# Attention and expert block on one core: an order of its own for the last unit, and its results taken out in halves

## The reference

```python
# x: (8, 1024, 256) float32; 16 heads of 16; RoPE on q and k
h = layernorm(x)
q, k, v = split(h @ Wqkv)                      # per head
num = exp(rot(q) @ rot(k).T / 4)               # numerators: rotated q, k
den = sum(exp(q @ k.T / 4), over all keys)     # denominators: plain q, k, all 1024 keys
attn = where(causal, num / den, 0)
x = x + (attn @ v) @ Wout + bout
h = layernorm(x)
shared = square(relu(h @ Ws1)) @ Ws2
logits = h @ Wr                                # 8 experts, top 2
prob = trunc(softmax(top two logits))          # 1 only where the softmax rounds to 1, else 0
x = x + shared + sum_e prob_e * (square(relu(h @ W1[e])) @ W2[e])
```

## Time and profile before

| | |
|---|---|
| median of 3 runs | 1724.95 us (1722.38 to 1730.55) |
| the profiled execution | 1729.71 us, of which the span of the trace is 1728.1 us |
| busy share of the span | ACT 92%, PE 88%, DVE 49%, POOL 30% |
| granted TensorE clock | 0.96 on the mean |
| last unit on ACT | 1631.79 to 1683.23 us |
| after the last exponential of scores | 1683.23 to 1728.1 us, 44.9 us |

### The profile page before, as it was taken

How to read it: one execution, slowest core, us unless ns; L and a number is a source line. 1 busy time by engine, 2 the same in 40 slices (tenths; PEclk the granted TensorE clock), 3 DMA queues, 4 the chain that set the end, 5 groups by cost and what they waited for, 6 DMA issues and landing times.

```text
span 1728.1 us, 25467 instructions
## 1 busy us (share of the span) xinstructions
PE 1517.6 (88%) x8224; PEld 588.5 (34%) x8224; DVE 852.2 (49%) x1946; ACT 1594.2 (92%) x2639; POOL 515.5 (30%) x865
## 2 busy tenths in 40 slices
PE   2988989899899989899898898999998999989985
PEld 1322323333333333333333333333333333333324
DVE  4434434754446554555446654456545554455215
ACT  1899999999999999999999999999999999999990
POOL 3223232422333232232333313332233323223110
PEclk8988999999999999999999999999999999999896
DMA  5332233331434314333333313343043332432200
GB/s 155 110 113 86 83 110 110 112 105 46 135 104 123 111 46 138 105 109 92 99 125 122 98 65 126 101 134 110 24 138 107 120 101 68 132 119 65 83 25 25
DMA packets 95005, 172.05 MB, mean 100 GB/s; under 512 B 15504, under 2 KB 82064, under 8 KB 82576
## 3 DMA queue, kind: packets, MB, share of 16 engines
q1 hardware_dynamic: 94272, 169.15, 31.5%
q10 hardware_dynamic: 592, 1.18, 0.3%
HBM read 111.55 MB, written 58.72 MB: 99 GB/s over the span
## 4 chain that ended last, share of the span: by engine, by line
ACT 66%; PE 15%; DVE 11%; issue 4%; DVEq 1%; POOL 1%; DMA 1%; SPq 0%; POOLq 0%
ACT scores L488 44%; ACT probs L498 19%; PE scores L544 4%; ACT probs L500 3%; PE side L602 3%; PE scores L551 3%; DVE rest L852 2%; PE y_ps L573 2%; DVE parts L850 2%; DVEq L789 1%; DVE raw L865 1%; DVE parts L856 1%; PE side L657 1%; DVE turned L870 1%; DVE rot L874 1%
## 5 line engine op out<-in xcount | busy, mean ns | idle before, releaser
L488 ACT ACTIVATE scores<-scores 128x1024 f32<-128x1024 f32 x1024 | 1051.5, 1041 | 37.8 <-PE scores L544 36.9
L544 PE MATMUL scores<-stack 96*128 96x512 bf16 x2048 | 591.4, 388 | 80.8 <-ACT scores L488 36.7
L498 ACT ACTIVATE probs<-scores 128x1024 f32<-128x1024 f32 x512 | 487.2, 1037 | 33.2 <-PE scores L551 32.6
L551 PE MATMUL scores<-stack 96*128 96x512 bf16 (+3 forms) x1536 | 337.1, 337 | 51.9 <-ACT scores L488 37.6
L394 POOL TENSOR_SCALAR_AFFINE_SELECT probs<-probs 128x256 f32<-128x256 f32 (+1 forms) x640 | 231.8, 387 | 426.4 <-ACT probs L498 304.8
L573 PE MATMUL y_ps<-probs,v_sb 128*32 128x512 f32 (+3 forms) x3072 | 332.8, 505 | 8.8 <-POOL probs L394 7.6
L544 PEld LDWEIGHTS scores<-stack 96*128 96x128 bf16 x2048 | 151.2, 98 | 514.1 <-ACT scores L488 236.3
L404 POOL TENSOR_TENSOR parts<-rest,parts 128x512 bf16<-128x512 f32 x124 | 143.2, 1154 | 314.7 <-DVE parts L856 314.7
L551 PEld LDWEIGHTS scores<-stack 96*128 96x128 bf16 x1536 | 124.4, 99 | 289.3 <-ACT scores L488 118.1
L488 ACT ACTIVATION_READ_ACCUMULATOR scores<-scores 128x1 f32 x1024 | 219.6, 214 | 0.0
L402 POOL TENSOR_TENSOR rot<-raw,cos_sb 128x512 f32<-128x512 f32 x62 | 89.4, 1442 | 398.1 <-DVEq L866 398.1
(11 more groups left out here) (121 smaller groups left out, 1082.8 us busy)
## 6 DMA issues: line engine op xcount, KB each, us to landing
stack<-qk_parts SPq DMA_DIRECT2D x762, 128.0 KB, 2.6
qk_parts<-parts SPq DMA_DIRECT2D x127, 384.0 KB, 2.6
out<-x_mid SPq DMA_DIRECT2D x32, 256.0 KB, 2.8
x_in<-in_L_attn_x SPq DMA_DIRECT2D x7, 1024.0 KB, 5.4
x_in<-in_L_attn_x SPq DMA_DIRECT2D x2, 512.0 KB, 4.4
stack<-qk_parts ACTq DMA_DIRECT2D x6, 128.0 KB, 4.6
probs<-in_L_attn_Wqkv SPq DMA_DIRECT2D x1, 512.0 KB, 5.7
cos_sb<-in_cos SPq DMA_DIRECT2D x1, 512.0 KB, 6.5
```

The costliest lines, as they stand in the source:

```text
L488: nc.scalar.activation(src, src, ACT.Exp, scale=SCALE, accum_out=den[:, g % 2, i, j:j + 1]).then_inc(exp_done, 1)
L498: nc.scalar.activation(probs[:, chunk % 2, j, :], src, ACT.Exp, scale=SCALE).then_inc(exp_done, 1)
L544: mm = nc.tensor.matmul(tile[:, half * HALF:(half + 1) * HALF], q[:, j, i * P:(i + 1) * P], k[:, j, half * HALF:(half + 1) * HALF], start= ...
L551: mm = nc.tensor.matmul(tile[:, col:col + n], k[:, h, i * P:(i + 1) * P], q[:, h, q0:q0 + n], start=True, stop=True)
```

## The change

**The last unit's order.** Unit 3 of batch 7 gets its own tables (`unit_of` gives it index 4): `ORDER_LAST` starts with numerators of chunk 0, and the first 16 denominators are those of the upper query blocks 4 to 7 (all four heads), the last 16 those of the lower. The upper ones are complete after step 31. Pieces with V, side work, reciprocals and branch have new steps; ffn 4 to 7 go to steps 0, 3, 8 and 17, the branch to 28.

**The upper half inside the unit.** The rest of batch 7 is now a list of 23 tiles, `END_TILES`, in halves. Its first five (norm 0, acc 2 and 3, t2 2 and 3, with the upper half's statistics and layernorm) run in `side` at steps 37, 38, 40, 47 and 49. The other 18 run after the unit, in an order that mixes both halves. The inverse root is now done twice, on 4 columns each. Logits are made in two halves.

**Outputs.** For batch 7 `send_out` does not wait for the branch any more; the pairs go out in the order 2, 3, 0, 1. If the branch is taken, DVE waits for those sends and POOL sends all four again; if not, POOL only raises `out_again`, for which SP waits at the very end.

```diff
+ORDER_LAST = [0, (0,), 4, (1,), 0, (2,), 7, (3,), 11, (4,), 10]
+STEPS = [unit_steps(ORDER, [("den", j, i) for j in range(HG) for i in range(NB)])] * G
+STEPS.append(unit_steps(ORDER_LAST, [("den", j, i) for half in (1, 0) for j in range(HG)
+                                     for i in range(half * NB // 2, (half + 1) * NB // 2)]))
+LAST_HIGH_DEN = max(s for s, x in enumerate(STEPS[G]) if x[0] == "den" and x[2] >= NB // 2)
+def unit_of(b, g):
+    return G if b == B - 1 and g == G - 1 else g
 PV_STEPS = [
...
+    (6, 9, 20, 21, 25, 29, 30, 31, 35, 44, 46, 48),
-TAKE_Y = [43, 43, 36, 48]
+TAKE_Y = [43, 43, 36, 48, 36]
 SIDE = [
...
+    {0: ("ffn", 4), 3: ("ffn", 5), 8: ("ffn", 6), 17: ("ffn", 7), 37: ("end", 0), 38: ("end", 1),
+     40: ("end", 2), 47: ("end", 3), 49: ("end", 4)},
+END_TILES = [("norm", 0), ("acc", 2), ("acc", 3), ("t2", 2), ("t2", 3), ("norm", 1), ("up", 2),
+             ("logits_t", 1), ("acc", 0), ("acc", 1), ("up", 3), ("down", 2), ("t2", 0), ("t2", 1),
+             ("logits", 1), ("down", 3), ("logits_t", 0), ("up", 0), ("up", 1), ("logits", 0), ("down", 0),
+             ("down", 1), ("routed", 0)]
+RECIPROCALS_LAST = (5, 35)
+BRANCH_LAST = 28
@@ sync @@
-                        send_out(b - 1, pair)
+                        send_out(b - 1, pair, pair)
...
-                sp.wait_ge(taken["gen"], at1(b, TILES["gen"], TILES["gen"]))
-                sp.sem_inc(held["sp"], 1)
+                if b < B - 1:
+                    sp.wait_ge(taken["gen"], at1(b, TILES["gen"], TILES["gen"]))
                 sp.dma_start(out_v[b][:, 2 * g:2 * g + 2, :], x_mid[:, 2 * g:2 * g + 2, :]).then_inc(out_sent, 16)
-            for g in range(G):
-                send_out(B - 1, g)
+            for n, pair in enumerate((2, 3, 0, 1)):
+                send_out(B - 1, pair, n)
             sp.wait_ge(out_sent, at1(B, 16 * G, 0))
+            sp.wait_ge(out_again, 16 * G)
@@ gpsimd, load_experts @@
+                    if b == B - 1:
+                        pool.wait_ge(taken["gen"], at1(b, TILES["gen"], TILES["gen"]))
+                        pool.wait_ge(out_sent, at1(B, 16 * G, 0))
+                        for pair in range(G):
+                            pool.dma_start(out_v[b][:, 2 * pair:2 * pair + 2, :], x_mid[:, 2 * pair:2 * pair + 2, :]
+                                           ).then_inc(out_again, 16)
                 with pool.Else():
                     pool.sem_inc(expert_loaded, 32 * E)
+                    if b == B - 1:
+                        pool.sem_inc(out_again, 16 * G)
@@ tensor @@
+            def end_tile(n, side):
+                what, t = END_TILES[n]
+                b = B - 1
+                if what == "norm":
+                    pe.wait_ge(spread_ready, at(b, 4, 2 + t + 1))
...
+                elif what == "acc":
+                    pe.wait_ge(end_taken, END_TILES.index(("norm", 1 - t // 2)) + 1)
...
+                elif what == "t2":
+                    pe.wait_ge(xn2_ready, at(b, 4, (t + 2) % 4 + 1))
...
+                elif what == "up":
+                    pe.wait_ge(end_taken, END_TILES.index(("t2", t)) + 1)
...
+                elif what == "down":
+                    pe.wait_ge(hidden_ready, at(b, 4, (t + 2) % 4 + 1))
...
+                mm.then_inc(end_full, 1)
...
+                if kind == "end":
+                    if t == 0:
+                        for k0, b0, n0 in before:
+                            pe.wait_ge(taken[k0], (at1 if k0 in ("ffn", "gen") else at)(b0, TILES[k0], n0 + 1))
+                    pe.wait_ge(end_taken, t)
+                    end_tile(t, side)
+                    return []
...
+            for n in range(IN_LOOP, len(END_TILES)):
+                pe.wait_ge(end_taken, n - 2 * RING + 1)
+                end_tile(n, bank(n))
@@ vector @@
+            def high_reciprocals(b, g):
+                dve.wait_ge(exp_done, at(b, G * NSTEP, g * NSTEP + LAST_HIGH_DEN + 1))
+                nc.vector.reciprocal(rden[:, NB // 2:NB, g % 2, :], den[:, g % 2, NB // 2:NB, :])
+                settle()
+            def low_reciprocals(b, g):
+                dve.wait_ge(exp_done, at(b, G * NSTEP, (g + 1) * NSTEP))
+                nc.vector.reciprocal(rden[:, 0:NB // 2, g % 2, :], den[:, g % 2, 0:NB // 2, :])
+                settle()
+            def end_tile(n, side):
+                what, t = END_TILES[n]
...
+                if what == "norm":
+                    spread_reciprocals((t,))
+                if what == "routed":
+                    route(b)
+                dve.wait_ge(end_full, n + 1)
...
+                elif what == "acc":
+                    if t == 2:
+                        dve.wait_ge(out_sent, at1(b, 16 * G, 0))
+                    blocks = slice(2 * t, 2 * t + 2)
+                    nc.vector.tensor_tensor(x_mid[:, blocks, :], side.rearrange("p (i d) -> p i d", i=2), x_acc[:, blocks, :],
+                                            ALU.add).then_inc(end_taken, 1)
+                    settle()
+                    block_stats(x_mid, t)
+                    if t % 2 == 1:
+                        layernorm_stats(1, 2 * t - 2, 2 * t + 2)
+                        for t0 in (t - 1, t):
+                            layernorm(x_mid, 1, t0, xn2_ready)
...
+                elif what == "down":
+                    y = x_mid[:, 2 * t:2 * t + 2, :]
+                    nc.vector.tensor_tensor(y, side.rearrange("p (i d) -> p i d", i=2), y, ALU.add).then_inc(end_taken, 1)
+                    dve.drain().then_inc(out_ready, 1)
...
-            reciprocals(last_b, G - 1)
-            spread_reciprocals()
...
+            low_reciprocals(last_b, G - 1)
+            for n in range(IN_LOOP, len(END_TILES)):
+                end_tile(n, bank(n))
             experts(last_b)
```

171 lines of the change are left out of this document (108 added, 63 removed).

## The result

| | before | after |
|---|---|---|
| median | 1724.11 us (1722.38 to 1730.55, 4 runs) | 1706.53 us (1704.58 to 1710.97, 4 runs) |
| ratio | 1 | 0.9895, interval 0.9863 to 0.9927 |
| the profiled execution | 1729.71 us, span 1728.1 | 1710.97 us, span 1709.4 |
| last unit on ACT, U | 51.44 us | 49.83 us |
| last exponential to the end of the last addition, A | 38.54 us | 24.35 us |

What follows compares the result with a forecast made beforehand. ACT was taken to set the pace up to the last exponential, then a tail of latency. Gains of 14.9 in the tail less 0.4 and 0 gave 14.5 us off the 1724.95 median: 1710.5, range 1704 to 1717.5.

Steps and rivals of the forecast that it cites:

- signs for "wrong": Last unit: ACT idle above 2 us, PE waiting over 2 us for DVE, or SP waiting long for POOL after landing.
- Last addition from 38.5 to 26.35: Tail behind the last exponential: half its work moves into the unit, so the last addition ends earlier, worth 12.2 us.
- I take the middle: Tail from up 0 on: a returning full clock would save about 2.0 us; 26.35 was taken instead of 27.35.
- all-half sum: Tail walked through with tiles at the half clock: the last addition ends 27.35 us behind the last exponential.
- clock kept in the tail: Rival: TensorE at full clock for most of the tail and ACT idling less, 4 us more gain, 1706; chance 0.10.
- The inverse root on 4 columns, 2.9 us: Tail on DVE: 12 instructions cost 2.9 us as before; scaling with width would make the tail 1.0 us shorter.
- Last addition to end, 6.3 to 3.6: End of the tail: three pairs sent earlier, the count and branch now last; worth 2.7 us.
- The unit, taken at 0 with ends -2 and +3: Last unit on ACT: possible clock-fall losses of 1 to 3 us against savings up to 2.2 us, taken as 0.
- Reciprocals 0 to 0.4 late, taken at 0.4: Unit's end on DVE: the take-over behind t2 3's copy makes the last reciprocals up to 0.4 us late.
- Paid back inside the unit: Rival: PE at half clock in steps 10 to 31, waiting on DVE, starves ACT by 5 to 7 us; 1717, chance 0.17.
- slower: Rival: half clock holds through the unit, 28 us lost against 14.5 won, 1738; chance 0.03.
- The upper half does not finish inside: Rival: late layernorm pushes t2 2 and 3 behind the last exponential, costing 3 to 4 us; 1714, chance 0.10.

Runs made afterwards that it cites:

- half_behind: Changed kernel with the five upper-half inner tiles run behind the unit, ahead of the other 18; median 1724.04 us, ratio 1.0005 to before.
- fill_both: Changed kernel with 8 unread matmuls ahead of norm 1 and 20 ahead of t2 0 in the tail; median 1707.84 us, ratio 0.9886 to before.
- sends_only: Kernel before with only the sends of batch 7 moved ahead of the branch; median 1726.12 us, ratio 1.0010 to before.
- sends_late: Changed kernel with its sends put behind the branch again; median 1710.74 us, ratio 0.9918 to before.
- ffn_late: Changed kernel with ffn 4 to 7 at steps 10, 13, 15 and 17 instead of 0, 3, 8 and 17; median 1708.12 us, ratio 0.9880.
- behind_fill: half_behind plus four unread matmuls at each of steps 37, 38, 40, 47 and 49; median 1719.98 us, ratio 0.9969 to before.
- acc_second: Changed kernel with acc 0 and 1 moved behind up 2 and ahead of the half logits tile; median 1702.61 us, ratio 0.9872 to before.

## Why the prediction was right, and where a term was off

The forecast was 1710.5 us in a range of 1704 to 1717.5; the time is 1706.53. The direction, the place of the gain and its two parts came out, and none of the signs for "wrong" appeared. One of the signs for "right" did not either, ACT idle near 2 us: it was 0.6 (U less the 49.2 of work). The gain was 3.1 us larger than forecast in the medians and 4.2 between the two profiled executions (18.7 for 14.5). The terms below are read from the traces; they add up to 4.1, and 0.1 lies ahead of the unit:

- **Last addition from 38.5 to 26.35.** It is 24.35. Up to DVE's first product the walk holds (2.58 us, 2.8 forecast). The queue ahead of acc 0 was under-sized: acc starts 5.05 us behind the last exponential, not 4.6. Up 2 took 1.84 us where I had 1.60. Half the logits took 1.56 (1684.97 to 1686.53) where I had halved 1.94 to 0.97, and the halving was a step that failed, not only a size: half_behind has this tile at a clock of 0.50 throughout (row below), and it takes 1.92 us, as long as the whole tile before. Here it was shorter only since the clock came back within it. But acc 0 and 1 ran at full clock, 1.99 for both and not 3.36, which made the statistics ready at 9.2 instead of 10.0. From the start of t2 to the last addition I had 12.2, with 1.0 of it taken off for the clock; it is 10.9, since up 0, up 1, down 0 and down 1 took 1.99 and 1.96 per pair, the full rate.
- **The clock in the tail.** "I take the middle" was the choice that failed in size. The work right behind each of PE's two long waits ran at half clock, and at about 1686 and 1700 the full clock was back; the mean is 0.77 against 0.65 before. The saving of 2.0 us from up 0 on, of which I took half, came whole: 10.9 us from t2 to the last addition, 13.2 by the all-half sum. Acc 0 and 1 brought 1.4 more. fill_both measured what a full clock through the whole tail would still bring, 2.9 us. The rival *clock kept in the tail*, 1706, is the nearest to the time, and it is half right: full for acc and the last four tiles, but half behind the waits of 2.95 and 4.70 us. The Trainium skill, "TensorE: Matmul & The Clock Gate", section "HAM oscillation", has gaps between bursts put the engine back to the half clock; this trace agrees at both long gaps (0.64 in 1681 to 1686, behind the 2.95 us, and 0.50 in 1694 to 1698, behind the 4.70) and shows no fall at the short waits up to 1706 (1.00 in 1702 to 1706, below). I had taken that section to mean that the all-half sum of 27.35 holds; 24.35 was measured, since the clock came back within both bursts.
- **The inverse root on 4 columns, 2.9 us.** It is 2.88 (1691.19 to 1694.07), 0.16 to 0.17 each, as with 8 columns. The rule of the Trainium skill, "VectorE: DVE Perf Modes", section on the TRN2 errata, that each instruction that reads SBUF pays a fixed extra latency, was the right one to keep; by scaling with width the tail would have been 1.0 us shorter. half_behind, with both roots in the tail, has a tail 1.4 to 2.8 us longer than that of the kernel with the old order and the new sends (42.19 and 40.84); it differs in the order of all its tiles too, so that is not the price of the root alone.
- **Last addition to end, 6.3 to 3.6.** 3.57. The count took 1.98 us where I had 1.7, and from its conversion (1707.81) to the end it is 1.59, forecast 1.49 and 0.4. So POOL's branch, taken at 0, adds nothing to the sum. The sum, 2.7, is what sends_only measured (2.8), but "worth" was too simple: in the changed order the same sends are worth 5.6 (sends_late).
- **The unit, taken at 0 with ends -2 and +3.** It is -1.6, near the lower end. I had the sentence for it, ffn 4 and 5 filling the steps at which the clock fell, and gave it no value. ffn_late puts that at 0.4 us at most, and half_behind with behind_fill put the 1.5 us at the inner tiles: their PE work, which I counted as a load on a slack of 2 us, is what keeps the clock up at the end of the unit. That piece had the wrong sign. The fall of the clock that I feared at steps 10 to 21 did come (0.65 in 1644 to 1648), and cost ACT 0.31 us, not 1 to 3.
- **Reciprocals 0 to 0.4 late, taken at 0.4.** 0: they start at 1681.52, 0.04 us behind the last exponential. t2 3 was through in time (1678.94).
- *Paid back inside the unit* (1717) and *slower* (1738) needed a PE that falls behind ACT. ACT stood 0.31 us. *The upper half does not finish inside* (1714) needed t2 3 behind the last exponential; it is 2.5 us ahead of it.

The half logits tile of half_behind, and the windows of after on which the point on the clock rests, PEclk third from the end, with the longest wait of PE in the second:

```profile
1697.22 1.92 PE L752 MATMUL scores<-xn2t,wr_sb 128*32 128x256 f32 x8
```
```profile
1681.48:1686.00 4.52, 3.51 (x14) 2.21 (x16) 2.27 (x6) 0.01 (x1) 0.00 (x0) 0.64 0.00 0
...
1690.00:1694.00 4.00, 0.25 (x2) 0.00 (x0) 3.02 (x18) 0.00 (x0) 0.00 (x0) 0.87 0.00 0
1694.00:1698.00 4.00, 3.05 (x13) 2.90 (x14) 3.70 (x9) 0.00 (x0) 0.00 (x0) 0.50 0.01 4
...
1702.00:1706.00 4.00, 2.52 (x12) 1.60 (x10) 3.27 (x12) 0.21 (x1) 0.00 (x0) 1.00 0.01 2
```

**What stays open.** The sends alone shorten Z by 2.8 us in both traces, and two timed comparisons do not show it in the median. And the start of the last unit wanders by 12 us between traces, by 10 of them between two on one chip (acc_second 1622.90, fill_both 1633.15); what moves it was not found.
